# Row-packed score matmuls: each head of a pair in its own half of TensorE's rows, on two PSUM banks at once

## The chip, the cores and the metric

One NeuronCore of a Trainium2 chip runs the whole program. The metric is the device time of one execution in microseconds, the median of several. Engines: PE is TensorE, DVE VectorE, ACT ScalarE, POOL GpSimd, SP SyncE, whose queue issues the DMAs.

## What is computed

Input x is 16 batches of 512 tokens of 256 values. The part that matters is the attention of 16 heads of 16 values each; the rest is cut.

```python
scores = jnp.take(causal_kern, jnp.maximum(doff, 0), axis=-1)
...
scores = scores + qm[..., :, None] + km[..., None, :]
qc = (x @ cq_w).reshape(Bq, Sq, H, CR).transpose(0, 2, 1, 3)
kc = (x @ ck_w).reshape(Bq, Sq, H, CR).transpose(0, 2, 1, 3)
scores = scores + MIX * jnp.einsum('bhic,bhjc->bhij', qc, kc) / math.sqrt(CR)
scores = jnp.where(causal, scores, -1000000000.0)
attn = jax.nn.softmax(scores, axis=-1)
ctx = jnp.einsum('bhij,bhjd->bhid', attn, v)
...
s = attention block with its FFN of 1024;  g = silu(FP4-rounded gated FFN of 704)
x = x + s * g
```

## The kernel before

A preparation (weights rounded to FP4 values and transposed, the positional kernel of all batches) is followed by a program over batches in three parts: a head (batch 0 and what must precede it), a loop over batches 1 to 14, and an end. Each engine runs a list of steps in an order written out by hand in the table `ORDER`, one string per engine and part, so that the work of three neighbouring batches is interleaved: the attention and the gated FFN of batch b, the output projection and the wide FFN of batch b-1, and the projections and the first half of the maxima of batch b+1. Steps wait for each other by counted semaphores (`Event`).

The score of a head is a bf16 matmul. Queries and keys (8 values a head) are split in three bf16 parts and laid out in 48 rows of products, with 6 more rows for the bias terms and, for the scores, 2 rows for a shift (minus the row maximum). A pair of heads shares one block of `KS` (keys): 2 x 54 rows. `QS` (queries) has one block per head, in which the other head's rows are zero, so that a matmul over 108 rows (L563, maxima) or 112 rows (L591 and L595, scores) gives one head's result. POOL zeroes QS at the end of the preparation (L1251).

The steps that the change touches:
- `mx.half.pair.unit`: raw scores of query tiles against all earlier keys, on PE (L563) into one of two banks (3 and 4) of PSUM. DVE reduces them to row maxima (L927, with a memset of an unused column, L922, ahead). A pair has five units in `MAXUNITS`, each of one bank: (512), (384 and 128), twice, and (256 and 256).
- `sc.pair.unit`: the transposed scores. A head has three units: its four own diagonal blocks of 128 columns (L591), and two of past blocks, 384 and 256+128 columns (L595). Each takes the next of two banks (0 and 1). ACT exponentiates them (L740 in place, L749 into `Pr`). The own blocks are then multiplied with the positional weights `Tz` by DVE (`muld`, L957), which is what frees their bank; the past blocks are multiplied by POOL (`mul`, L1062) in SBUF.
- `pv`: probabilities times values of four heads (L611), fp32, four heads on four strips of 32 columns of the array, into one bank.
- `load`: SP loads KS and QS of half of the pairs from DRAM, six DMAs (L492). `mio` brings the shift rows.

Other PE steps go to four more banks. L683 and L692 are the wide FFN, L635 and L650 the gated one, L665 the output projection, L542 and L550 the projections of x, L571 the transposes of the shifts.

The waits for a bank look like this (before): a score unit waits for the one two units ago.

```python
n = 6 * p + u
ago = n - len(SC_BANKS)
```

Of the kernel before, what the change touches and what calls it, by code (L numbers as in the profile page):

```python
# [40 lines left out]
KROWS = 2 * (HROWS + BROWS)  # L41
SHIFT = 2
SROWS = KROWS + 2 * SHIFT
# [1524 lines left out]
```

How the kernel before makes its waits and increments, by code:

```python
    def wait(self, eng, b, k=None):  # L63
        if isinstance(b, int) and b < 0:
            return
        k = self.per - 1 if k is None else k
        eng.wait_ge(self.sem, b * (self.per * self.by) + (k + 1) * self.by)
# [1125 lines left out]
        def prologue_sync(sp):  # L1194
            sp.dma_start(freqs, w["waves"]).then_inc(L["waves"], 16)
            sp.dma_start(pos, w["positions"]).then_inc(L["waves"], 16)
            for i in range(NX):
                sp.dma_start(x_in[i][:], x_b[i]).then_inc(x_sem[i], 16)
            sp.wait_ge(L["zero"], N_MEMSETS)
            for dst, src in zero_list:
                sp.dma_start(dst, src).then_inc(L["consts"], 16)
            for dst, src in load_list:
                sp.dma_start(dst, src).then_inc(L["weights"], 16)
            with sp.Fori(1, B // NX) as n:
                for i in range(NX):
                    sp.wait_ge(L["pool"], n * NX + (i - NX + 1))
                    sp.dma_start(x_in[i][:], x_b[n * NX + i]).then_inc(x_sem[i], 16)
            sp.dma_start(rows_d.rearrange("b h n -> (b h) n").rearrange("(p a) n -> p a n", a=2)[:, :, S:ROW],
                         zeros.rearrange("p (a n) -> p a n", a=2)).then_inc(L["rows"], 16)
            sp.wait_ge(L["exp"], 1)
            for g in range(4):
                sp.dma_start(rows_d[:, g::4, 0:S], dens[32 * g:32 * g + B]).then_inc(L["rows"], 16)
            sp.wait_ge(L["ready"], 5)
            sp.dma_start(qb_d[:, 0:3, :], KS[0:H, 0:3, :]).then_inc(L["ones"], 16)
```

## Time and profile before

| | |
|---|---|
| median of 3 runs | 2038.28 us (2036.96 to 2039.29) |
| the profiled execution, its own time | 2039.16 us |
| its span, first to last instruction | 2037.4 us |
| busy: PE, DVE, POOL, ACT | 1852.7, 1611.7, 1106.1, 900.0 us |
| mean granted clock of TensorE | 0.959 of full speed |

Busy time counts the time in which at least one instruction of an engine runs. A matmul's duration holds its passage through the array, so durations of neighbouring matmuls overlap; what a matmul costs the next is read from start to start. "PEld" rows are weight loads. "issue" is time in which nothing that the profile shows was waited for.

### The profile page before, as it was taken

Reading aid. Unit: us, or ns where it says so; the run is one execution under the profiler, and the core shown is the slowest. Engines: PE = TensorE matmul, PEld = TensorE weight load, DVE = VectorE, ACT = ScalarE, POOL = GpSimd, SP = SyncE. Lnnn points to the kernel's source line nnn. Section 1 sums busy time; section 2 is a strip of 40 time slices with the busy share of each in tenths; the row PEclk is TensorE's granted clock in tenths of the full one; section 3 lists DMA queues with packets and bytes.
Section 4 is the critical chain, followed back from the end, with each engine's and each line's share of the span. In section 5 each row is a group of like instructions: output and inputs, shape, how many; then the busy total and the mean of one; then the engine's idle time right before and its main releaser. Section 6 shows DMA issues by size and latency. Waiting matters only on the chain.

```text
span 2037.4 us, 41650 instructions
## 1 busy us (share of the span) xinstructions
PE 1852.7 (91%) x12508; PEld 1316.0 (65%) x12508; DVE 1611.7 (79%) x5186; ACT 900.0 (44%) x1814; POOL 1106.1 (54%) x788
## 2 busy tenths in 40 slices
PE   4745789999999999999999999999999999999996
PEld 1222356767676776767676767767676767677765
DVE  5863987888888888978888888889788888888752
ACT  0111345445453635454454536354544545364532
POOL 1223464746564665747465646657474656466471
PEclk7757899999999999999999999999999999999998
DMA  7204122323232222223232322232232323222110
GB/s 215 85 11 111 36 79 71 114 71 102 60 102 70 86 68 86 87 70 112 70 102 60 103 70 85 68 87 87 70 112 70 102 60 101 72 84 68 52 64 21
DMA packets 129139, 165.32 MB, mean 81 GB/s; under 512 B 9821, under 2 KB 90718, under 8 KB 129028
## 3 DMA queue, kind: packets, MB, share of 16 engines
q1 hardware_dynamic: 129034, 164.29, 28.0%
q14 instruction: 84, 0.69, 0.1%
q8 instruction: 21, 0.34, 0.1%
HBM read 127.85 MB, written 36.41 MB: 81 GB/s over the span
## 4 chain that ended last, share of the span: by engine, by line
PE 57%; DVE 13%; issue 12%; POOL 5%; ACT 2%; DMA 1%; DVEq 0%; ACTq 0%; POOLq 0%; SPq 0%
PE ps L692 10%; PE ps L683 10%; PE ps L635 8%; PE ps L542 4%; PE ps L650 4%; PE ps L563 3%; PE ps L665 3%; PE ps L595 3%; POOL Pr L1062 3%; PE ps L550 2%; PE ps L611 2%; PE ps L591 2%; DVE st L859 2%; DVE nmax L927 2%; POOL slot L1094 1%
## 5 line engine op out<-in xcount | busy, mean ns | idle before, releaser
L1062 POOL TENSOR_TENSOR Pr<-Pr,Tz 128x768 f32<-128x768 f32 (+2 forms) x384 | 478.2, 1274 | 251.6 <-ACT Pr L749 249.8
L927 DVE CUSTOM_DVE_ANT_0 ps<-ps,future 128x512 f32<-128x512 f32 (+3 forms) x1024 | 474.8, 517 | 50.1 <-issue 49.7
L749 ACT ACTIVATE Pr<-ps 128x384 f32<-128x384 f32 x512 | 243.3, 489 | 373.7 <-PE ps L595 371.0
L683 PE MATMUL ps<-catT,w 128*128 128x256 f32 x1024 | 237.3, 380 | 0.7 <-ACT catT L810 0.7
L563 PE MATMUL ps<-KS,QS 108*128 108x512 bf16 (+3 forms) x1024 | 220.6, 306 | 17.2 <-DVE nmax L927 11.4
L692 PE MATMUL ps<-w,gT 128*128 128x256 f32 x1024 | 233.0, 381 | 0.9 <-ACT gT L821 0.9
L740 ACT ACTIVATE ps<-ps 128x512 f32<-128x512 f32 x256 | 150.4, 587 | 147.9 <-PE ps L591 145.9
L957 DVE SCALAR_TENSOR_TENSOR Pr<-ps,Tz 128x512 f32<-128x512 f32 x256 | 175.2, 685 | 46.7 <-ACT ps L740 40.3
L692 PEld LDWEIGHTS ps<-w,gT 128*128 128x128 f32 x1024 | 190.9, 190 | 25.8 <-ACT gT L821 1.3
L683 PEld LDWEIGHTS ps<-catT,w 128*128 128x128 f32 x1024 | 189.7, 190 | 26.7 <-ACT catT L810 1.0
L635 PE MATMUL ps<-wgT,xqT 128*128 128x352 f32 x512 | 178.7, 472 | 3.6 <-DVE slot L994 2.9
L650 PE MATMUL ps<-wdT,hqT 128*128 128x256 f32 x768 | 178.5, 382 | 0.9 <-ACT hqT L786 0.9
L595 PE MATMUL ps<-QS,KS 112*128 112x384 bf16 (+2 forms) x768 | 161.9, 275 | 19.0 <-DVE Pr L957 14.2
L635 PE MATMUL ps<-wuT,xqT 128*128 128x352 f32 x512 | 174.6, 464 | 0.0
L1094 POOL TENSOR_TENSOR slot<-slot 128x704 f32<-128x704 f32 x64 | 107.7, 1683 | 99.6 <-DVE slot L849 99.6
L1100 POOL TENSOR_TENSOR rstd<-ve,minus_half 128x4 f32<-128x4 f32 x32 | 32.6, 1019 | 232.9 <-DVE ve L867 231.4
L650 PEld LDWEIGHTS ps<-wdT,hqT 128*128 128x128 f32 x768 | 142.7, 190 | 20.4 <-ACT hqT L786 1.4
L611 PE MATMUL ps<-Pr,v_cur 128*17 128x128 f32 (+2 forms) x3584 | 151.0, 319 | 0.1
L563 PEld LDWEIGHTS ps<-KS,QS 108*128 108x128 bf16 x1024 | 88.0, 98 | 92.3 <-DVE nmax L927 41.6
L927 DVE DVE_READ_ACCUMULATOR2_ANT nmax<- 128x1 f32 x1024 | 144.0, 141 | 0.0
L635 PEld LDWEIGHTS ps<-wuT,xqT 128*128 128x128 f32 x512 | 98.2, 192 | 55.2 <-issue 1.7
L611 PEld LDWEIGHTS ps<-Pr,v_cur 128*17 128x17 f32 x3584 | 94.6, 97 | 52.1 <-issue 39.4
(214 smaller groups left out, 3262.1 us busy)
## 6 DMA issues: line engine op xcount, KB each, us to landing
Tz<-kernel_rows SPq DMA_DIRECT2D x128, 512.0 KB, 3.8
KS<-k_parts SPq DMA_DIRECT2D x32, 384.0 KB
QS<-q_parts SPq DMA_DIRECT2D x64, 192.0 KB
hY<-in_x SPq DMA_DIRECT2D x20, 512.0 KB, 4.9
xn<-in_x SPq DMA_DIRECT2D x20, 512.0 KB, 3.5
out<-y SPq DMA_DIRECT2D x16, 512.0 KB, 3.0
q_parts<-q_sp SPq DMA_DIRECT2D x16, 384.0 KB, 2.8
k_parts<-k_sp SPq DMA_DIRECT2D x16, 384.0 KB, 2.4
```

The source lines that it names most:

```text
L563: ins = mm(o, QS[0:KROWS, 2 * p + e, it * P:(it + 1) * P], KS[0:KROWS, p, 0:n], start=True, stop=True)
L595: ins = mm(dst[:, at:at + PAST[j]], KS[0:SROWS, p, j * P:(j + 1) * P], rhs[:, S - 1:P * (j + 1) - 1:-1], start=True, stop=True)
L611: ins = mm(dst[32 * hh:32 * hh + HD + 1, to:to + n], v_cur[:, j, 4 * g + hh, :], rhs[:, n - 1::-1], start=i == 0, stop=i == len(pieces) - 1)
L635: ins = mm(dst[:, 0:IH], xqT[:, c, t * P:(t + 1) * P], wt[:, c, f * IH:(f + 1) * IH], start=c == 0, stop=c == KD - 1)
L650: ins = mm(dst[:, 0:D], hqT[:, c * P:(c + 1) * P], wdT[:, c, :], start=c == 0, stop=c == KI - 1)
L683: ins = mm(dst[:, i * n:(i + 1) * n], w1[:, c, f * P:(f + 1) * P], catT[:, c, hf * n:(hf + 1) * n], start=c == 0, stop=c == KD - 1)
L692: ins = mm(dst[:, 0:D], gT[:, f, at:at + P], w2[:, f, :], start=f == 0, stop=f == KF - 1)
L740: inc(af(src, src, ACT.Exp), "a_exp")
L749: inc(af(Pr[:, p % 4, e, at:at + wd], src[:, 0:wd], ACT.Exp), "a_exp")
L927: ins = v.tensor_tensor_reduce(o, o, future[:, S - n:S], -1.0, 3e38, ALU.add, ALU.min, nmax[:, 2 * pl + e, it:it + 1])
L957: v.scalar_tensor_tensor(blocks(Pr[:, p % 4, e, 0:S]), blocks(ps[:, SC_BANKS[n % len(SC_BANKS)], :]), 3e38, near, ALU.min, ALU.mult).then_ ...
L1062: ins = g.tensor_tensor(a, a, Tz[:, p % 2, :, P * j:P * j + PAST[j]], ALU.mult)
```

## The change

Each head of a pair gets rows of its own: the first rows 0 to 55, the second rows 64 to 119, in both QS and KS. QS has one block per pair, without zeros. A matmul takes 54 (maxima) or 56 rows (scores) at row 0 or 64, and the two heads' matmuls of a block are written one after the other. The unit of a step is now a pair: it takes two banks, one per head, and counts one PE event at its last matmul. A pair has three units of maxima (512; 384 and 128; 256; each for both heads) and three of scores (own; 384; 256+128). ACT and DVE count an event per bank. Ring lengths stay: two banks for scores, two for maxima. The loads are eight DMAs a half. POOL's memset of QS is gone. The table `ORDER` is another one for all engines and parts.

```diff
-KROWS = 2 * (HROWS + BROWS)
+KROWS = HROWS + BROWS
 SHIFT = 2
-SROWS = KROWS + 2 * SHIFT
+SROWS = KROWS + SHIFT
+HALF_ROWS = P // 2
...
-MAXUNITS = [[(0, 3)], [(0, 2), (0, 0)], [(1, 3)], [(1, 2), (1, 0)], [(0, 1), (1, 1)]]
+MAXUNITS = [[3], [2, 0], [1]]
+NM, NS = len(MAXUNITS), 1 + len(UNITS)
...
-        QS = sb("QS", [P, H, S], BF16)
+        QS = sb("QS", [P, PAIRS, S], BF16)
...
-        NLOAD = 6
+        NLOAD = 8
...
                     for e in range(2):
-                        r0, r1 = e * HROWS, 2 * HROWS + e * BROWS
-                        loads += [(QS[r0:r0 + HROWS, heads, :][:, e::2, :], rows(qs_d, 2 * CR)[r0:r0 + HROWS]),
-                                  (QS[r1:r1 + BROWS, heads, :][:, e::2, :], rows(qb_d, 2)[e * BROWS:(e + 1) * BROWS])]
+                        r = HALF_ROWS * e
+                        for t, parts_d, bias_d in ((KS, ks_d, kb_d), (QS, qs_d, qb_d)):
+                            loads += [(t[r:r + HROWS, pairs, :], rows(parts_d, 2 * CR)[e * HROWS:(e + 1) * HROWS]),
+                                      (t[r + HROWS:r + KROWS, pairs, :], rows(bias_d, 2)[e * BROWS:(e + 1) * BROWS])]
...
-                    dst = b_bank(s)
+                    dst = []
                     at = 0
-                    for e, it in MAXUNITS[u]:
+                    for it in MAXUNITS[u]:
                         n = (it + 1) * P
-                        o = dst[:, at:at + n]
-                        ins = mm(o, QS[0:KROWS, 2 * p + e, it * P:(it + 1) * P], KS[0:KROWS, p, 0:n], start=True, stop=True)
+                        for e in range(2):
+                            if len(dst) == e:
+                                dst.append(b_bank(s + (e,)))
+                            r = slice(HALF_ROWS * e, HALF_ROWS * e + KROWS)
+                            ins = mm(dst[e][:, at:at + n], QS[r, p, it * P:(it + 1) * P], KS[r, p, 0:n], start=True, stop=True)
                         at += n
                     inc(ins, "pe_max")
...
+                    for j in range(T) if u == 0 else UNITS[u - 1]:
+                        wd = P if u == 0 else PAST[j]
+                        hi, lo = (P * j + P - 1, P * j - 1) if u == 0 else (S - 1, P * (j + 1) - 1)
+                        for e in range(2):
+                            if len(dst) == e:
+                                n = 2 * (NS * p + u) + e
+                                ago = n - len(SC_BANKS)
...
+                                if ago // 2 % NS == 0:
+                                    v_mul[ago % 2].wait(pe, hb, ago // 2 // NS)
+                                else:
+                                    E["a_exp"].wait(pe, hb, ago)
+                                dst.append(ps[:, SC_BANKS[n % len(SC_BANKS)], :])
+                            r = slice(HALF_ROWS * e, HALF_ROWS * e + SROWS)
+                            rhs = QS[r, p, hi::-1] if lo < 0 else QS[r, p, hi:lo:-1]
+                            ins = mm(dst[e][:, at:at + wd], KS[r, p, j * P:(j + 1) * P], rhs, start=True, stop=True)
+                        at += wd
                     inc(ins, "pe_sc")
...
-            g.memset(QS[:].rearrange("p h s -> p (h s)").bitcast(F32), 0.0).then_inc(L["ready"], 1)
```

Two places of the loop show how the order moves on PE. In the rows, KS and QS are the score operands, `v_max` tells that DVE has read a maxima bank, `a_exp` that ACT has read a score bank, `v_mul0` and `v_mul1` that DVE's product has freed one.

PE, the last stretch of the loop before the change: maxima of the last two pairs (L563), P times V (L611) between them.

```order
L563 MATMUL ps<-KS,QS 128x512 [waits v_max]
...
L563 MATMUL ps<-KS,QS 128x384 [waits v_max]
L563 MATMUL ps<-KS,QS 128x128
L611 MATMUL ps<-Pr,v_cur 17x384 [waits g_mul,v_gs,v_mul1,a_vcopy]
L611 MATMUL ps<-Pr,v_cur 17x384 x3
L611 MATMUL ps<-Pr,v_cur 17x256 x4
L611 MATMUL ps<-Pr,v_cur 17x128 x20
...
L563 MATMUL ps<-KS,QS 128x512 [waits v_max]
```

PE, the same stretch now: L543 are the maxima, L575 the scores, L590 P times V.

```order
L575 MATMUL ps<-QS,KS 128x384 [waits v_mul0]
L575 MATMUL ps<-QS,KS 128x384 [waits v_mul1]
...
L543 MATMUL ps<-KS,QS 128x384 [waits v_max]
...
L543 MATMUL ps<-KS,QS 128x384 [waits v_max]
L543 MATMUL ps<-KS,QS 128x128 x2
L575 MATMUL ps<-QS,KS 128x256 [waits a_exp] x2
L575 MATMUL ps<-QS,KS 128x128 x2
...
L543 MATMUL ps<-KS,QS 128x256 [waits v_max]
...
L543 MATMUL ps<-KS,QS 128x512 [waits v_max]
...
L543 MATMUL ps<-KS,QS 128x384 [waits v_max]
...
L590 MATMUL ps<-Pr,v_cur 17x384 [waits g_mul,v_gs,v_mul1,a_vcopy]
```

Units of two banks stand one behind another here, each waiting for the banks of the one before. (Of the last three units the second head's rows are left out at "...".)

PE, early in the loop, before the change:

```order
L591 MATMUL ps<-QS,KS 128x128 [waits a_exp]
L591 MATMUL ps<-QS,KS 128x128 x3
...
L673 MATMUL ps<-ident,hY 128x128 x3
...
L595 MATMUL ps<-QS,KS 128x384 [waits a_exp]
...
L563 MATMUL ps<-KS,QS 128x384 [waits v_max]
L563 MATMUL ps<-KS,QS 128x128
...
L595 MATMUL ps<-QS,KS 128x256 [waits v_mul0]
```

and now:

```order
L575 MATMUL ps<-QS,KS 128x128 x6
...
L652 MATMUL ps<-ident,hY 128x128 x3
...
L543 MATMUL ps<-KS,QS 128x512 [waits v_max]
...
L575 MATMUL ps<-QS,KS 128x384 [waits v_mul0]
L575 MATMUL ps<-QS,KS 128x384 [waits v_mul1]
...
L543 MATMUL ps<-KS,QS 128x384 [waits v_max]
...
L575 MATMUL ps<-QS,KS 128x256 [waits a_exp]
```

The scores of 384 columns now wait for both products of the unit just before; before, they had a bank that was one unit older. Runs of score and maxima matmuls alternate with full-array work as they did.

## Rows read from the trace of the kernel before

**Rows 1.** the page, busy times (share, instructions) and PE's busy tenths in 40 slices
```profile
PE 1852.7 (91%) x12508; PEld 1316.0 (65%) x12508; DVE 1611.7 (79%) x5186; ACT 900.0 (44%) x1814; POOL 1106.1 (54%) x788
...
PE   4745789999999999999999999999999999999996
```

**Rows 2.** windows of one batch each, all engines; first line: the columns
```profile
core 0: us, PE busy (x) PEld busy (x) DVE busy (x) ACT busy (x) POOL busy (x), PEclk, DMA share, GB/s
...
983.60:1095.70 112.10, 108.66 (x766) 79.37 (x765) 93.73 (x305) 54.99 (x110) 66.30 (x47) 1.00 0.28 83
...
sum 560.50, PE 543.29 PEld 396.56 DVE 468.60 ACT 274.98 POOL 331.44; mean PE 108.66 PEld 79.31 DVE 93.72 ACT 55.00 POOL 66.29
```

**Rows 3.** timeline of PE: start us, us, instructions, idle before
```profile
1007.40 1.89 PE L683 MATMUL ps<-catT,w 128*128 128x256 f32 x8
1009.13 0.60 PE L563 MATMUL ps<-KS,QS 108*128 108x512 bf16 x3
1009.57 1.95 PE L683 MATMUL ps<-catT,w 128*128 128x256 f32 x8
...
1011.79 0.49 PE L595 MATMUL ps<-QS,KS 112*128 112x384 bf16 x3
1012.21 2.36 PE L611 MATMUL ps<-Pr,v_cur 128*17 128x384 f32 x56
1014.50 0.40 PE L591 MATMUL ps<-QS,KS 112*128 112x128 bf16 x4
```

**Rows 4.** weight loads by shape: count, busy us, mean ns, idle before
```profile
L692 PEld LDWEIGHTS ps<-w,gT 128*128 128x128 f32 x1024 | 190.9, 190 | 25.8 <-ACT gT L821 1.3
...
L611 PEld LDWEIGHTS ps<-Pr,v_cur 128*17 128x17 f32 x3584 | 94.6, 97 | 52.1 <-issue 39.4
...
L563 PEld LDWEIGHTS ps<-KS,QS 108*128 108x128 bf16 x1024 | 88.0, 98 | 92.3 <-DVE nmax L927 41.6 <-issue 11.8 <-DVE v_new L911 3.4
```

**Rows 5.** timeline of all engines, handoffs of score units
```profile
1000.46 0.69 DVE L957 SCALAR_TENSOR_TENSOR Pr<-ps,Tz 128x512 f32<-128x512 f32 x1
...
1001.20 0.34 PE L595 MATMUL ps<-QS,KS 112*128 112x256 bf16 x2 [0.45 <-DVE Pr L957]
1001.28 0.89 ACT L749 ACTIVATE Pr<-ps 128x384 f32<-128x384 f32 x2
...
1001.85 0.40 PE L591 MATMUL ps<-QS,KS 112*128 112x128 bf16 x4 [0.31 <-ACT Pr L749]
...
1002.28 0.58 ACT L740 ACTIVATE ps<-ps 128x512 f32<-128x512 f32 x1
```

**Rows 6.** timeline of DVE, maxima one behind another
```profile
1082.76 0.72 DVE L927 CUSTOM_DVE_ANT_0 ps<-ps,future 128x512 f32<-128x512 f32 x1
...
1083.41 0.59 DVE L927 CUSTOM_DVE_ANT_0 ps<-ps,future 128x384 f32<-128x384 f32 x1
...
1083.92 0.33 DVE L927 CUSTOM_DVE_ANT_0 ps<-ps,future 128x128 f32<-128x128 f32 x1
...
1084.18 0.46 DVE L927 CUSTOM_DVE_ANT_0 ps<-ps,future 128x256 f32<-128x256 f32 x1
...
1084.55 0.14 DVE L927 DVE_READ_ACCUMULATOR2_ANT nmax<- 128x1 f32 x1
```

**Rows 7.** waits of PE and its loads, one batch: us, times, longest
```profile
PE ps L595 <- DVE Pr L957: 0.7, 2, 0.4
...
PEld ps L595 <- DVE Pr L957: 1.6, 3, 0.7
PEld ps L563 <- DVE nmax L927: 1.5, 5, 0.5
```

**Rows 8.** timeline of the end of the preparation
```profile
152.05 3.51 POOL L1251 MEMSET QS<- 128x4096 f32 x1
...
156.19 0.18 DVE L1383 MEMSET slot<- 128x64 f32 x2 [7.08 <-ACT wdT L1467]
...
159.99 0.35 SPq L1217 DMA_DIRECT2D q_bias_parts<-KS  x1
```

More of the change, by code:

```diff
@@ L180 @@
         sync="""
-            last:T.0 last:load.1 last:T.1 last:T.2 last:T.3 last:mio.1 last:T.4 last:T.5 last:T.6 last:T.7 last:fin
+            last:T.0 last:load.1 last:T.1 last:T.2 last:T.3 last:T.4 last:mio.1 last:T.5 last:T.6 last:T.7 last:fin
             tail:fin
@@ L279, in b_uses @@
 def b_uses(s):
-    return [s] if s[0] in ("xT", "proj", "v", "mx", "mT") else []
+    return [s + (e,) for e in range(2)] if s[0] == "mx" else [s] if s[0] in ("xT", "proj", "v", "mT") else []
 def build(nc, x_d, w, out_d):
@@ L500, in sync_steps @@
                     for e in range(2):
[L501 to L503 removed]
+                        r0 = HALF_ROWS * e + KROWS
+                        sp.dma_start(QS[r0:r0 + SHIFT, HALF * half:HALF * (half + 1), :], sd[e]
+                                     ).then_inc(d_shift[half].sem, 16)
                 elif k == "T":
@@ L914, in vector_steps @@
                     _, half, pl, u = s
-                    E["pe_max"].wait(dve, half_batch(half, b), 20 * half + 5 * pl + u)
-                    src = bank(b_plan, s)
+                    E["pe_max"].wait(dve, half_batch(half, b), (half * HALF + pl) * NM + u)
                     if pl == 0 and u == 0:
@@ L921, in vector_steps @@
                             E["v_m"].wait(dve, b, 3)
-                    v.memset(turn[:, 20 * half + 5 * pl + u:20 * half + 5 * pl + u + 1], 0.0)
-                    at = 0
-                    for e, it in MAXUNITS[u]:
-                        n = (it + 1) * P
-                        o = src[:, at:at + n]
-                        ins = v.tensor_tensor_reduce(o, o, future[:, S - n:S], -1.0, 3e38, ALU.add, ALU.min,
-                                                     nmax[:, 2 * pl + e, it:it + 1])
-                        at += n
-                    inc(ins, "v_max")
+                    n0 = (half * HALF + pl) * NM + u
+                    v.memset(turn[:, n0:n0 + 1], 0.0)
+                    for e in range(2):
+                        src = bank(b_plan, s + (e,))
+                        at = 0
+                        for it in MAXUNITS[u]:
+                            n = (it + 1) * P
+                            o = src[:, at:at + n]
+                            ins = v.tensor_tensor_reduce(o, o, future[:, S - n:S], -1.0, 3e38, ALU.add, ALU.min,
+                                                         nmax[:, 2 * pl + e, it:it + 1])
+                            at += n
+                        inc(ins, "v_max")
                 elif k == "mfin":
@@ L933, in vector_steps @@
                     hb = half_batch(half, b)
-                    E["v_max"].wait(dve, hb, 20 * half + 19)
+                    E["v_max"].wait(dve, hb, 2 * (half + 1) * HALF * NM - 1)
                     if half:
```

295 lines of the change are left out of this document (124 added, 171 removed).

## Prediction

> **What bounds the kernel now.** I read the page's busy shares and slices first, then the windows of one batch, then PE's groups by shape, then the timeline of PE. The page: PE is busy 91% of the span, DVE 79%, and from slice 7 on PE's digit is 9 [rows 1]. Batches 1 to 14 run in one loop. Its period is 112.10 us, the same in each window; of it PE is busy 108.7, DVE 93.7, ACT 55.0, POOL 66.3, and the granted clock is 1.00, the upper level of 2.4 GHz, 0.417 ns a column [rows 2]. So PE sets the batch, with 3.4 us in which nothing at all is in flight on it.
>
> The score matmuls are bf16 and stream a column a clock: three of them (512, 384 and 128 columns) start at 1009.13 and the next matmul at 1009.57, 0.44 us for 1024 columns [rows 3]. A head has 1280 columns of maxima (L563) and 1280 of scores (L591, L595), a batch 16 x 2560 = 40960 columns = **17.1 us of PE's 112.1**.
>
> **Does packing overlap at all?** The trace has one packed case. P times V (L611) puts four heads on four column strips: 56 passes of 128 to 384 columns end in 2.36 us [rows 3]. One head alone is 1280 columns, in two passes at two clocks a column (fp32; L683 x8 of 256 columns takes 1.73 us to the next start, 0.84 ns a column [rows 3]), 2.13 us. So four strips cost what one does, and I take it that two row halves do likewise: **-8.5 us a batch**. Bounds: 0 (they serialize), and -8.5.
>
> Weights could forbid it, since each matmul has a load of its own. A bf16 load of 128 columns takes 98 ns, no more than an fp32 one of 17 columns (97); an fp32 one of 128 takes 190 [rows 4], 0.84 ns a column over the 17. So 97 ns is nearly all latency, an fp32 load of 128 streams in about 107 ns and the bf16 one in some 15. Two bf16 loads fit behind the shortest pair (53 ns) if row halves keep that speed.
>
> **What it costs on PE: switches.** Where PE goes from full-array matmuls to strips of 32 columns and back, time is lost. L595 x3 starts at 1011.79 with 768 columns (0.32), P times V starts at 1012.21, not 1012.11; its last column passes near 1014.41 (1012.21 + 2.13, and about 5 ns for each of its 14 steps), and L591 starts at 1014.50. Both ways 0.095 us, against under 0.01 us between full-array matmuls of any two kinds (1009.13 to 1009.57) [rows 3]. The 14 switches of a batch before (four P times V, two transposes of shifts, one 32-column projection) are 1.3 us. In the changed kernel every run of maxima or scores is in a third shape, 64 rows by 128 columns. Counted down the order, the loop has 60 changes of shape where it had 14, because these runs are short and lie between full-array work: 46 x 0.095 = **+4.4 us a batch**; bounds 0 (row halves switch free) and +4.4. The Trainium skill, "TensorEngine Tiling (Array Packing)", Key Properties, says that changing the tiling mode, not just the tile, drains TensorE. By that rule row halves pay like strips, and the trace agrees for strips; without it the sum would be lower by 4.4 us a batch.
>
> **What it costs in waits: rings of one.** Before, a score unit took one of banks 0 and 1, a maxima unit one of 3 and 4: PE filled one while ACT or DVE emptied the other. Now a unit takes both banks, so PE's next unit of that kind waits until the last is emptied, and the consumer then waits for PE. From rows: four matmuls of 128 columns (L591 at 1001.85) last 0.40 where their columns need 0.22, so a result is 0.17 late; ACT starts 0.03 after it (1002.25, 1002.28), PE 0.05 after DVE (1001.15, 1001.20); ACT takes 0.58 for 512 columns, 0.89 for two units of 384, DVE's product 0.69 [rows 5]. DVE's maxima take from start to start 0.65 for 512 columns, 0.51 for 384, 0.26 for 128, 0.37 for 256, and 0.14 for the last readout [rows 6]. From PE's last column to the release of the second bank this makes 1.7 us (512), 1.9 (384 and 128), 1.2 (256), 1.2 (scores of 384) and 2.3 (own-block scores with the product; 1.6 for the first bank). PE's own work between two units of a kind must be that long. At the loop's end it isn't. Scores 256+128 follow 0.2 after the unit they reuse: wait 1.0. Then maxima 256 wait 0.75, maxima 512 wait 1.2, maxima 384+128 wait 1.7: together 4.7 us within three runs. Near the start, scores 384 after own-block scores and maxima 384+128 wait 1.6 more, other places 0.8. Walking the whole order so, with DVE and ACT free whenever wanted, gives 7.1 us; the same walk down the order of before, with two banks in turn, 1.4. **+5.7 us a batch**, bounds +3 (handoffs quicker, waits that swallow a switch) and +8 (DVE late as well).
>
> The trace of before has such waits, small: in one batch PE's weight loads are held 1.6 us for DVE's products and 1.5 for its maxima, and of the first only 0.7 shows on PE itself [rows 7]; the rest lies behind the ends of running matmuls. DVE's lateness adds about 2 us to the walk's 1.4 before; I assume the same afterwards, since DVE has as much to do (40 memsets become 24, -1 us, hidden: DVE isn't the bound). ACT and POOL do the same work. SP issues 8 loads a half instead of 6, with the same bytes; no wait of PE for a DMA is among the waits of a batch [rows 7], so I cost it at nothing, and if that cover went it would be the issue of four DMAs a batch.
>
> **Outside the loop.** POOL's memset of QS goes (3.51 us); behind it stand the memset of KS, that of v_new, and at 159.99 the first DMA that waits for them. DVE's memset ends at 156.4, so this DMA moves by 3.4 [rows 8]: **-3.4 us**, once. Batch 0 and batch 15 lie in the head and end: each -8.5 for pairs, +2.4 and +3.7 for 25 and 38 more switches. In the head the first half's maxima run with DVE back to back, and a round trip of some 0.45 us for each of 12 units comes on top (+5); the end has ring waits like a batch. I put both at 0, bounds -6 and +6 each.
>
> **Sum.** A batch: -8.5 + 4.4 + 5.7 = +1.6 (I take +1.5: 0.1 for switches swallowed in waits). 14 x 1.5 = +21, less 3.4: +17.6 on the profiled execution's 2039.16 us, which lies inside the runs of before (median 2038.28): **2056 us**, +0.9%.
>
> **Rivals.**
> 1. *Faster: the waits stay small.* The order is new for all engines, and other work may cover the round trips (DVE has 18 us idle a batch [rows 2]); then a batch is 112.1 - 8.5 + 4.4 = 108.0, and with -3.4 and -6 in each of head and end the time is 2039 - 57 - 15 = 1967. It decides where ring waits grow by less than 4.1 us a batch. For it: before, PE's own wait for DVE's products is 0.7 us a batch [rows 7]. Against: at the loop's end the four units stand almost side by side and no cover is in the order. If switches are free as well, another 62 off: 1905.
> 2. *Pairs overlap only in part.* If row halves lose the fast bf16 load, a pair with loads of 107 ns each lasts at least 214 ns: 48 pairs of 128 columns go from 112 to 214 (+4.9), 16 of 256 stay, 16 of 384 gain 1.7, 8 of 512 gain 1.7: a batch +1.5 where I have -8.5, 2056 + 160 = 2216, somewhat less as PE's slower pace fills waits. With plain serial pairs: +8.5 x 16 = 136, 2190.
> 3. *Slightly partial overlap*, a quarter of the 8.5 lost: +34, 2090. The Trainium skill, "TensorE: Matmul & The Clock Gate", Packing small matmuls, gives 3.07 times for four row tiles of 512 columns; at that efficiency two give 1.54 instead of 2, and the sum would be 6.0 for pairs in place of 8.5, some 40 us more. No run here shows it; the strips of L611 show none of it.
> 4. *The change doesn't do what it says*: the matmuls of a pair might stand apart. The order shows them next to each other, each with its own bank's wait. I give it nothing of its own.
>
> **Chances.** Forecast (2035 to 2080) 0.5; rival 1 in some strength 0.31; rival 3 0.1; rival 2 0.09. The likeliest gives the time. Two in ten left out, the range reaches half way into rival 1 and over rival 3: **1985 to 2100**. A measurement here tells 0.2% (4 us) from no change. Faster 0.31, same 0.08, slower 0.61. The forecast's own range is 2035 to 2080.
>
> **What would show it.** Overlap: the starts of a pair's two matmuls under 0.02 us apart, and a pair of 512 columns 0.22 us to the next start. Switches: 0.095 us between the last pair's columns and a full-array matmul, some 60 times a batch. Rings: PE or its loads waiting for DVE's maxima by 3 to 6 us a batch, most of it in the last 12 us of the loop. DVE busy near 93 us of a longer period. q_bias_parts' first DMA near 156.6. I'm wrong if the period is under 111.9, if a pair's starts lie a whole stream apart, or if switches of 64-row shapes cost nothing.

## The result: 3.2% slower, and the profile after

The changed kernel takes **2104.42 us** (median of 4 runs, 2099.68 to 2105.24) against 2038.78 (2036.96 to 2039.46) of the kernel before on the same chip: ratio 1.0319, 95% interval 1.0301 to 1.0336. Slower was forecast, but by 18 us, not 66; the time lies just above the range.

The profiled execution took 2104.96 us, its span is 2103.1. The page, to be held against [rows 1]:

```profile
PE 1883.8 (90%) x12508; PEld 1230.9 (59%) x12508; DVE 1597.2 (76%) x4930; ACT 924.6 (44%) x1844; POOL 1095.3 (52%) x787
...
PEclk8757689999999999999999999999999999999998
...
L543 PE MATMUL ps<-KS,QS 54*128 54x512 bf16 (+3 forms) x1024 | 188.2, 322 | 70.7 <-DVE nmax L907 68.5
```

PE is 31 us busier, though its columns are fewer; its maxima (L543) wait 68.5 us for DVE, where those of the kernel before (L563) waited 11.4. The slices' clock digit still reads 9 all through the loop, which hides what follows. Three batches, beside [rows 2]:

```profile
core 0: us, PE busy (x) PEld busy (x) DVE busy (x) ACT busy (x) POOL busy (x), PEclk, DMA share, GB/s
1008.10:1124.00 115.90, 110.44 (x765) 74.00 (x765) 92.95 (x289) 56.55 (x113) 65.89 (x47) 0.97 0.30 80
1124.00:1241.00 117.00, 111.55 (x766) 74.52 (x766) 92.89 (x289) 56.61 (x113) 65.91 (x47) 0.96 0.29 80
1241.00:1356.70 115.70, 110.24 (x765) 73.52 (x766) 92.81 (x289) 56.55 (x113) 65.93 (x47) 0.97 0.29 81
```

The period is 116.2 in the mean of 14 (1627.1 us) where it was 112.1 (1569.7), and **the granted clock is 0.96 or 0.97 where it was 1.00**. Cut into stretches of 6.8 us at the loop's end, the same view shows where (the last row is the 3.4 us just ahead of the fall):

```profile
1105.80:1112.60 6.80, 4.92 (x25) 2.58 (x24) 6.13 (x25) 2.13 (x5) 4.95 (x4) 1.00 0.00 0
1112.60:1119.40 6.80, 5.80 (x62) 3.10 (x63) 5.17 (x20) 0.20 (x1) 5.09 (x4) 0.50 0.00 1
1119.40:1126.20 6.80, 5.89 (x37) 4.48 (x36) 2.28 (x10) 3.26 (x7) 1.45 (x1) 1.00 0.24 81
...
1109.20:1112.60 3.40, 1.75 (x9) 0.48 (x7) 3.20 (x17) 1.39 (x4) 2.74 (x3) 1.00 0.00 0
```

For 6.8 us TensorE runs at the lower of its two levels (0.50, 1.2 GHz), once in every batch; in 4 of the 14 a second fall of 3.4 us follows near the loop's start. In the 3.4 us ahead of the fall shown PE was busy for 1.75. PE's timeline over the place:

```profile
1108.82 0.39 PE L543 MATMUL ps<-KS,QS 54*128 54x384 bf16 x3 [0.23 <-DVE nmax L907]
...
1110.18 0.28 PE L543 MATMUL ps<-KS,QS 54*128 54x256 bf16 x1 [0.45 <-DVE nmax L907]
1110.95 0.28 PE L543 MATMUL ps<-KS,QS 54*128 54x256 bf16 x1 [0.49 <-DVE nmax L907]
1111.82 0.77 PE L543 MATMUL ps<-KS,QS 54*128 54x512 bf16 x2 [0.59 <-DVE nmax L907]
1113.45 1.25 PE L543 MATMUL ps<-KS,QS 54*128 54x384 bf16 x4 [0.86 <-DVE nmax L907]
1114.67 4.47 PE L590 MATMUL ps<-Pr,v_cur 128*17 128x384 f32 x56
```

Each maxima unit waits until DVE has emptied both banks of the last. These are the ring waits that were forecast, at the place that was forecast. What was not: the clock falls among them, and P times V (56 passes, L590) takes 4.47 us where it takes 2.36 [rows 3].

**The ledger of a batch.** All kernels below are compared in one way: over the 14 loop batches, the time from each matmul's start to the next is split into its columns at full clock; what is over at a change of shape, up to 0.105 us (switches); what is over otherwise by more than 0.02 us (waits); and what a stretch at half clock adds (clock). Such a stretch is called a fall below. Us a batch; the four add up to the period within 0.1.

| kernel | columns | switches | waits | clock | period | run, us |
|---|---|---|---|---|---|---|
| before | 103.9 | 1.4 | 6.9 | 0 | 112.1 | 2038.8 |
| changed | 96.1 | 5.8 | 11.3 | 3.0 | 116.2 | 2104.4 |
| full_paired | 103.5 | 1.4 | 10.0 | 2.3 | 117.2 | 2124.3 |
| light_max | 95.7 | 5.8 | 12.0 | 2.5 | 116.1 | 2089.7 |
| light_mul | 96.0 | 5.8 | 11.3 | 2.8 | 116.0 | 2103.2 |
| light_both | 95.8 | 5.8 | 9.7 | 1.5 | 112.8 | 2046.7 |
| full_light | 103.6 | 1.4 | 9.9 | 1.9 | 116.8 | 2109.3 |
| full_both | 103.7 | 1.4 | 7.9 | 0.2 | 113.2 | 2057.3 |
| before_both | 103.8 | 1.4 | 5.9 | 0 | 111.1 | 2014.0 |
| before_slow | 103.9 | 1.4 | 8.0 | 0 | 113.2 | 2056.8 |
| before_slower | 103.8 | 1.4 | 9.9 | 0.6 | 115.8 | 2101.5 |
| halves_single | 98.4 | 7.8 | 19.9 | 3.7 | 129.9 | 2310.4 |
| spread_end | 96.3 | 6.0 | 12.6 | 4.2 | 119.0 | 2145.7 |
| spread_both | 96.0 | 6.2 | 18.2 | 7.4 | 127.9 | 2270.6 |
| early7 | 96.3 | 6.1 | 13.7 | 3.1 | 119.3 | 2150.1 |
| sc7_early | 96.1 | 6.1 | 14.9 | 7.9 | 125.1 | 2234.3 |

The periods are those of the profiled execution, the last column is the median of all; for before_slower the two lie apart, since its profiled execution took 2087.3, the fastest of five, and the others had a lower mean clock (0.953 to 0.955 against 0.959). The clock column is the least certain: in the changed kernel batches with 10.2 us at half clock last 117.0 to 117.5 and those with 6.8 last 115.7 to 116.0, some 1.1 us for 3.4, by which the 7.8 us a batch at half clock would cost 2.5 and not 3.0.

So the change moves a batch by -7.8 (columns) + 4.4 (switches) + 4.4 (waits) + 3.0 (clock) = +4.1, 57 us over the loop. The rest of the 65.7 us between the two spans lies behind it: from the loop's end to the last instruction 165.9 us against 156.9, and 310.1 against 310.8 ahead of the loop's first whole batch.

### The profile page after: what moved, and what is told of

Read it like the earlier page. It is cut to its first block, busy times and chain, and to the rows that moved or that the text cites. A ratio compares the mean times of both kernels' runs of the same rounds, so it can differ in the third digit from the quotient of the medians.

```text
span 2103.1 us, 40843 instructions
## 1 busy us (share of the span) xinstructions
PE 1883.8 (90%) x12508; PEld 1230.9 (59%) x12508; DVE 1597.2 (76%) x4930; ACT 924.6 (44%) x1844; POOL 1095.3 (52%) x787
## 4 chain that ended last, share of the span: by engine, by line
PE 59%; DVE 20%; issue 10%; ACT 1%; DVEq 0%; POOL 0%; DMA 0%; ACTq 0%; POOLq 0%; SPq 0%
PE ps L662 11%; PE ps L671 11%; PE ps L590 7%; DVE ps L907 6%; PE ps L614 6%; PE ps L629 4%; PE ps L519 4%; PE ps L575 3%; PE ps L644 3%; PE ps L527 3%; PE ps L543 2%; DVE nmax L907 2%; PE ps L622 2%; DVE slot L974 2%; DVE Pr L937 2%
## 5 line engine op out<-in xcount | busy, mean ns | idle before, releaser
L727 ACT ACTIVATE Pr<-ps 128x384 f32<-128x384 f32 x512 | 222.7, 487 | 296.2 <-PE ps L575 294.9
L543 PE MATMUL ps<-KS,QS 54*128 54x512 bf16 (+3 forms) x1024 | 188.2, 322 | 70.7 <-DVE nmax L907 68.5
L662 PE MATMUL ps<-catT,w 128*128 128x256 f32 x1024 | 246.5, 393 | 0.3 <-ACT catT L788 0.3
L1068 POOL TENSOR_TENSOR slot<-slot,sc_h 128x704 f32<-128x704 f32 x64 | 88.9, 1389 | 273.9 <-DVE sc_h L816 273.9
L937 DVE SCALAR_TENSOR_TENSOR Pr<-ps,Tz 128x512 f32<-128x512 f32 x256 | 168.4, 685 | 23.3 <-ACT ps L723 20.5
L575 PE MATMUL ps<-QS,KS 56*128 56x128 bf16 (+2 forms) x1792 | 166.7, 248 | 21.6 <-DVE Pr L937 11.7
L590 PE MATMUL ps<-Pr,v_cur 128*17 128x128 f32 (+2 forms) x3584 | 183.8, 364 | 0.1
L723 ACT ACTIVATE ps<-ps 128x512 f32<-128x512 f32 x256 | 137.3, 579 | 86.0 <-PE ps L575 85.7
L543 PEld LDWEIGHTS ps<-KS,QS 54*128 54x128 bf16 x1024 | 54.6, 95 | 179.3 <-DVE nmax L907 130.2
L590 PEld LDWEIGHTS ps<-Pr,v_cur 128*17 128x17 f32 x3584 | 106.8, 109 | 76.7 <-issue 63.5
```

The lines of the kernel that those rows point to most:

```text
L543: ins = mm(dst[e][:, at:at + n], QS[r, p, it * P:(it + 1) * P], KS[r, p, 0:n], start=True, stop=True)
L575: ins = mm(dst[e][:, at:at + wd], KS[r, p, j * P:(j + 1) * P], rhs, start=True, stop=True)
L590: ins = mm(dst[32 * hh:32 * hh + HD + 1, to:to + n], v_cur[:, j, 4 * g + hh, :], rhs[:, n - 1::-1], start=i == 0, stop=i == len(pieces) - 1)
L662: ins = mm(dst[:, i * n:(i + 1) * n], w1[:, c, f * P:(f + 1) * P], catT[:, c, hf * n:(hf + 1) * n], start=c == 0, stop=c == KD - 1)
L723: inc(af(src, src, ACT.Exp), "a_exp")
L727: inc(af(Pr[:, p % 4, e, at:at + wd], src[:, 0:wd], ACT.Exp), "a_exp")
```

## The experiments

Two theories stood after the first trace. **A**: the clock falls after waits of PE that lie close together, whatever makes them; the row halves have no part in it. **B**: it falls because of work in row halves, with its 60 changes of shape. Lines of code and of order are shortened in the edits below; "..." marks what is left out.

### 1. The new order without row halves (full_paired)

```diff
-KROWS = HROWS + BROWS
+KROWS = 2 * (HROWS + BROWS)
...
-r = slice(HALF_ROWS * e, HALF_ROWS * e + KROWS)
-ins = mm(dst[e][:, at:at + n], QS[r, p, it * P:(it + 1) * P], KS[r, p, 0:n], start=True, stop=True)
+ins = mm(dst[e][:, at:at + n], QS[0:KROWS, 2 * p + e, it * P:(it + 1) * P], KS[0:KROWS, p, 0:n],
```

> The changed kernel's order, its two-bank units and its rings of one, but the score operands have all 128 rows again (108 or 112 used, a head's other rows zero), so no pair overlaps and the loop has 14 changes of shape as before. Theory A (the time that my sum missed is a lower granted clock, which follows the short waits of PE at the loop's end; the row halves have no part in it): PE's granted clock falls to half here too, once or twice a batch after those waits; a batch is 103.9 of columns + 1.4 of switches + 10 to 11 of waits + 2.6 to 3.9 of clock = 118 to 120 us (116.1 in the changed kernel, 112.1 before), 2120 to 2150 us in all. Theory B (the clock falls because of the work in row halves, with its 60 changes of shape): no fall in the loop, a batch of 115.5 to 116.5, 2085 to 2100 us.

2124.33 us, ratio 1.0432 (1.0414 to 1.0449), a batch of 117.2. At the loop's end, the timeline and two windows:

```profile
1236.20 0.28 PE L542 MATMUL ps<-KS,QS 108*128 108x256 bf16 x1 [0.62 <-DVE nmax L907]
1236.96 0.28 PE L542 MATMUL ps<-KS,QS 108*128 108x256 bf16 x1 [0.48 <-DVE nmax L907]
1237.84 0.77 PE L542 MATMUL ps<-KS,QS 108*128 108x512 bf16 x2 [0.59 <-DVE nmax L907]
1239.47 1.36 PE L542 MATMUL ps<-KS,QS 108*128 108x384 bf16 x4 [0.86 <-DVE nmax L907]
```

```profile
1232.30:1239.10 6.80, 4.31 (x22) 2.22 (x20) 6.10 (x26) 2.13 (x5) 5.59 (x4) 1.00 0.00 0
1239.10:1245.90 6.80, 6.29 (x64) 3.37 (x65) 4.53 (x18) 0.60 (x1) 5.00 (x4) 0.50 0.00 1
```

The same waits with 108 rows, and the same fall of 6.8 us (3.4 in 5 of the 14 batches). B is refuted for the clock; A stands, its batch somewhat below the 118 to 120 expected. The order and the two-bank units together cost 5.1 us a batch (waits +3.1, clock +2.3); row halves give 1.0 of it back. No run takes the new order apart from the rings of one: that these waits come from the rings rests on the rows above, where each unit waits for DVE to empty the banks of the one before.

### 2. Row halves in the order of before (halves_single)

```diff
-MAXUNITS = [[(0, 3)], [(0, 2), (0, 0)], [(1, 3)], [(1, 2), (1, 0)], [(0, 1), (1, 1)]]
+MAXUNITS = [[(0, 3)], [(0, 2), (0, 0)], [(1, 3)], [(1, 2), (1, 0)], [(0, 1)], [(1, 1)]]
...
-rhs = QS[0:SROWS, 2 * p + e, :]
+r = slice(HALF_ROWS * e, HALF_ROWS * e + SROWS)
+rhs = QS[r, p, :]
...
-ins = mm(dst[:, at:at + PAST[j]], KS[0:SROWS, p, j * P:(j + 1) * P],
+ins = mm(dst[:, at:at + PAST[j]], KS[r, p, j * P:(j + 1) * P],
```

> The order of the kernel before, a unit of one head in one of two banks in turn, but with each head's operands on a row half of its own (54 and 56 rows from row 0 or 64); the maxima unit that held blocks of both heads is split in two. The loop has 81 changes of shape where it had 15, and only where units of two heads stand side by side can they overlap. Both theories: 66 x 0.095 = +6.3 us a batch for the switches, 0 to -1.5 for neighbours that overlap, +0 to +1 for the waits. Theory A (clock follows the waits): clock stays at 1.00 in the loop, a batch of 117 to 119 us, 2110 to 2135 us in all. Theory B (clock follows row halves): it falls to half for some 7 us a batch or more, a batch of 120 to 123 us, 2150 to 2190 us. If a switch costs less where nothing overlaps, the batch is under 115.

2310.40 us, ratio 1.1348 (1.1329 to 1.1367). Switches came out as expected (7.8 against 1.4, 0.097 each). Two things did not. Columns fell by 5.5, far more than I allowed: a unit of one head starts while another head's is running, whatever their kinds. In this timeline of PE score units of the two heads both start at 1326.45, and a maxima matmul at 1326.62 runs beside a score matmul at 1326.63:

```profile
1326.45 0.28 PE L598 MATMUL ps<-QS,KS 56*128 56x256 bf16 x1 [0.24 <-DVE Pr L960]
1326.45 0.28 PE L594 MATMUL ps<-QS,KS 56*128 56x128 bf16 x2
...
1326.62 0.27 PE L565 MATMUL ps<-KS,QS 54*128 54x256 bf16 x1
1326.63 0.22 PE L594 MATMUL ps<-QS,KS 56*128 56x128 bf16 x1
...
1332.35 0.61 PE L565 MATMUL ps<-KS,QS 54*128 54x512 bf16 x1 [5.39 <-DVE nmax L930]
```

And waits rose to 19.9, as I read it for a reason of my own making: the split unit makes six units a pair out of five, so PE gets only two shorter units ahead of DVE, and here it waits 5.39 us through a long stretch of DVE's other work. (In that batch PE also waits 1.1 us for a load of QS.) The run tells nothing of the clock apart from waits (both are high), and only the switch price and the overlap are to be kept from it.

### 3. Moving the waits apart by order (spread_end, spread_both)

```diff
-dn.1 sc.7.0 mx.0.1.2 ctxt.2 tr.2.1 mx.0.2.0 dn.2 sc.7.1 mx.0.2.1 sc.7.2 mx.0.2.2 mx.0.3.0 mx.0.3.1 pv.3 tr.3.0 tr.3.1 mx.0.3.2 ctxt.3 dn.3
+dn.1 sc.7.0 mx.0.1.2 ctxt.2 tr.2.1 mx.0.2.0 sc.7.1 mx.0.2.1 sc.7.2 dn.2 mx.0.2.2 mx.0.3.0 pv.3 mx.0.3.1 tr.3.0 tr.3.1 ctxt.3 mx.0.3.2 dn.3
```

(dn is the down projection of the gated FFN and tr the transposes ahead of it, hr the rounding of its hidden values, f1 the first product of the wide FFN, ctxt a transpose behind P times V.) spread_both also has `mx.1.1.0 f1.0.0 sc.1.1 mx.1.1.1 f1.0.1 sc.1.2 xT.0 xT.1 sc.2.0` near the start.

> The changed kernel with only PE's order at the loop's end written otherwise: dn.2 stands behind the second and third of the last five maxima units, pv.3 between the fourth and the fifth, so fewer units stand side by side. Theory A: the waits there fall by 1 to 2 us a batch, and the clock no longer falls at the loop's end (2.6 to 3.4 us a batch given back): a batch of 111 to 113 us, 2035 to 2065 us in all. Theory B: the clock falls as before, at the same place or another: a batch of 114 to 115, 2075 to 2095 us. A third way: the waits only move to the product of POOL that pv.3 needs, and neither falls: 2095 to 2110.

> As the last one, and the tight place near the loop's start (four score and maxima units around hT) is spread with f1.0.0, f1.0.1 and the two transposes of x as well. Theory A: another 0.8 us of waits and the second, shorter fall of the clock (3.4 us of half clock in some batches) go: 1 to 2 us a batch below spread_end, a batch near 110.5, 2020 to 2050 us in all, level with the kernel before or faster. Theory B: only the waits fall, 2065 to 2085 us.

2145.65 (ratio 1.0543, 1.0524 to 1.0562) and 2270.64 (1.1112, 1.1051 to 1.1172): both far above every band. sc.7.1, put ahead of dn.2, waits 2.2 us for DVE's product of the last pair, because DVE does 1.9 us of hr.3 between the two products of that pair; near the start f1.0.0 waits 2.4 us a batch for a bank that DVE's gate product (slot, L973) has still to empty, and a maxima unit behind it 3.8 for ACT's eviction of the transposed x. The waits rose, and the clock with them (4.2 and 7.4 a batch). The versions don't test what they were made for; in them the two rose together, but light_max below shows that this is no rule.

### 4. Shorter waits without touching PE (light_max, full_light)

```diff
-o = src[:, at:at + n]
-ins = v.tensor_tensor_reduce(o, o, future[:, S - n:S], ...)
+o = src[:, at:at + P]
+ins = v.tensor_tensor_reduce(o, o, future[:, S - n:S - n + P], ...)
```

In light_max DVE takes the row maxima over the first 128 columns of each block alone; the maxima over its other columns are left out. full_light is full_paired with the same edit.

> The changed kernel with every instruction of PE, ACT and POOL as it is; DVE's maxima read 128 columns of each block in place of its 128 to 512, so a part of the maxima is left out. Per head DVE's reductions fall by 0.4 (512), 0.25 (384) and 0.1 (256) us, the ring of one is released that much sooner. Theory A (the clock follows PE's waits): waits fall from 11.4 to 8 or 9 us a batch and the clock no longer falls: 96.2 + 5.8 + 8.5 = 110.5 to 111.5 us a batch (116.1 in the changed kernel), 2025 to 2045 us in all. If the clock falls all the same with the waits gone (it follows what PE executes): 113 to 114.5 a batch, 2060 to 2085 us.

> The same light maxima in the kernel with full-array operands of the first experiment (117.2 us a batch there). With waits and clock out of the way the two differ by pairs and switches alone: -7.3 of columns and +4.5 of switches in row halves make a batch 3 us longer here than in light_max. Theory A: clock 1.00, 103.5 + 1.4 + 8 = 113 to 114 us a batch, 2055 to 2080 us in all, 35 to 50 us over light_max. If the difference is under 15 us, switches or pairs are mis-sized.

2089.67 (1.0258, 1.0238 to 1.0277) and 2109.27 (1.0354, 1.0334 to 1.0373). DVE is busy 82.4 us a batch in place of 92.9, and the period of light_max stays at 116.1. PE's and POOL's timeline at the loop's end of light_max:

```profile
1446.68 0.64 PE L543 MATMUL ps<-KS,QS 54*128 54x512 bf16 x2 [0.45 <-DVE nmax L907]
1447.78 0.64 PE L543 MATMUL ps<-KS,QS 54*128 54x384 bf16 x4 [0.46 <-DVE nmax L907]
1451.13 4.47 PE L590 MATMUL ps<-Pr,v_cur 128*17 128x384 f32 x56 [2.71 <-POOL Pr L1042]
```

```profile
1446.81 4.07 POOL L1042 TENSOR_TENSOR Pr<-Pr,Tz 128x768 f32<-128x768 f32 x3 [0.59 <-ACT Pr L727]
```

PE reaches its last maxima unit 2 us sooner (103.3 us into the batch, not 105.4) and then waits 2.7 us for **POOL's product of the last pair**, the second chain: scores, exp, DVE's product, scores again (their ring is of one too), exp, POOL. In the changed kernel it ended at 1114.41, 0.26 before P times V started; the maxima waits hid it. My expectation had one chain only: light_max lies 45 us above its band, full_light 29, and the two are 20 us apart, not 35 to 50. In light_max the waits are more than in the changed kernel (12.0 against 11.3) and the clock costs less (2.5 against 3.0), so the sum of the waits doesn't set the clock.

### 5. Both chains shortened, or the second alone (light_both, light_mul)

```diff
-for j in range(T - 1):
+for j in range(1 if p == 7 else T - 1):
```

light_both is light_max with this line in POOL's product, which leaves out two of its three parts for the last pair of each batch; light_mul has this line alone.

> light_max again, and POOL's product of the last pair of a batch is made for the first of its three parts only (the other two left out), so both things that PE waits for at the loop's end are short: in light_max PE went through the maxima sooner and then waited 2.8 us for that product, and a batch stayed at 116.0. Theory (two chains end there together, DVE's maxima by rings of one and scores, exp, product of the last pair; each hides the other): waits fall from 12.0 to 8 or 9 us a batch and, the waits being what the clock follows, the clock stays at 1.00: 110 to 112 us a batch, 2005 to 2035 us in all. If the clock follows what PE executes, 2.5 more a batch, 2045 to 2070. If a third chain stands behind, over 2075.

> The changed kernel with the full maxima and that short product of POOL. By the same theory the maxima alone hold PE to the same point (in the changed kernel the product ended at 1114.41 and PE's last maxima matmul at 1114.6): waits 10 to 11.4 a batch, clock falling as before, 115 to 116.1 us a batch, 2085 to 2104 us in all. If the product was what bound and the maxima only filled its time: under 113 a batch, under 2065.

2046.68 (1.0048, 1.0031 to 1.0065) and 2103.23 (1.0327, 1.0309 to 1.0344). The product alone gives nothing, the maxima alone 15 us, both 58 (the chips differ; by the ratios 13 and 55): two chains of nearly equal length end at P times V. With PE's instructions unchanged, 11.3 us of waits become 9.7 and the fall of 6.8 us becomes one of 3.4:

```profile
1428.80:1541.40 112.60, 108.64 (x765) 73.03 (x764) 81.61 (x289) 56.46 (x113) 64.07 (x45) 0.98 0.31 83
```

So the clock isn't set by what PE executes alone; shorter waits gave half of the fall back. It didn't come back to 1.00 as A had it: waits of 2.8 us in all are still there in the 8 us ahead of P times V. And though 11 us of DVE's and 2 of POOL's work are gone, it is still slower than before.

### 6. Waits put into the kernel before (before_slow, before_slower)

```diff
+if half == 0 and pl == 3:
+    at0 = 80 * e + 4 * it * (it + 1)
+    for i in range(8 * (it + 1)):
+        v.memset(slow[:, at0 + i:at0 + i + 1], 0.0)
 ins = v.tensor_tensor_reduce(o, o, future[:, S - n:S], ...)
```

That is before_slower; before_slow has 2 * it + 3 of them, in the last two pairs.

> The kernel before with one thing added: ahead of the maxima of the last two pairs of a batch DVE also writes 3, 5, 7 or 9 single columns of zeros, 5 to 6 us more of DVE's time in the last stretch of the loop. PE's instructions, their order, the full array and the two banks in turn stay. Theory A (waits of PE close together lower the clock, whatever makes them): PE waits 3 to 5 us more a batch and the clock falls to half there for some 7 us, 2.5 to 3.4 us more: a batch of 118 to 120.5 us, 2120 to 2155 us in all. A rival (the clock falls only with the changed order or with two-bank units): clock 1.00, a batch of 115 to 117, 2080 to 2110 us.

> As before_slow (which cost only 1.1 us of waits a batch and no clock), but stronger and in one place: in the last pair of a batch alone DVE writes 8 columns of zeros, some 0.06 us each, for each 128 columns of maxima that it then reads, 9 to 10 us more in the last five maxima units. Theory A (waits of PE close together lower the clock whatever makes them): 5 to 7 us more of waits and the clock at half for 3.4 to 7 us, 1.5 to 3.4 us more: a batch of 119 to 123 us, 2130 to 2185 us in all, with full-array operands, two banks in turn and the order of before. Rival (the new order or the two-bank units lower it): clock 1.00, 117 to 119 a batch, 2105 to 2135 us.

2056.82 (1.0095, 1.0075 to 1.0115) and 2101.47 (1.0325, 1.0308 to 1.0343). Two banks in turn swallow most of it: waits +1.1 and, in the usual batch of before_slower, +2.3, at clock 1.00. But in 6 of its 14 batches the period is over 116, and in these six, and in no other, the clock falls for 3.4 us:

```profile
1119.00:1238.80 119.80, 110.33 (x766) 80.22 (x765) 98.63 (x465) 55.22 (x110) 66.76 (x47) 0.99 0.27 78
1238.80:1353.20 114.40, 108.73 (x765) 79.36 (x764) 96.18 (x465) 54.95 (x110) 66.22 (x47) 1.00 0.28 82
```

The batch ahead of these two:

```profile
1114.33 0.39 PE L572 MATMUL ps<-ident_bf,sh_sp 128*16 128x128 bf16 x4 [1.78 <-DVE sh_sp L947]
1114.65 4.54 PE L651 MATMUL ps<-wdT,hqT 128*128 128x256 f32 x12
```

Here the clock falls at 1115.0, behind waits of 0.88 (at 1109.66) and 1.78 us, and the down projection takes 4.54 us; two more batches fall so. In the other three, each the next one behind such a batch, it falls about where a single wait of 3.54 us for hY ends. All with full-array operands, one-bank units and the order of before: the rival of this run is refuted. The size was under what I expected.

But the second batch of the two windows has the same two waits and no fall (clock 1.00):

```profile
1345.53 0.39 PE L564 MATMUL ps<-KS,QS 108*128 108x384 bf16 x2 [0.88 <-DVE nmax L932]
...
1350.20 0.39 PE L572 MATMUL ps<-ident_bf,sh_sp 128*16 128x128 bf16 x4 [1.78 <-DVE sh_sp L947]
```

So A holds in its weak form: waits can bring the fall in any of these kernels, and the same waits don't always.

### 7. The last candidates for a better version (early7, sc7_early)

```diff
-muld.7.0 hr.3 muld.7.1 mx.0.2.0 ...          DVE
+muld.7.0 muld.7.1 mx.0.2.0 hr.3 ...
-... mx.0.2.0 dn.2 sc.7.1 mx.0.2.1 sc.7.2 mx.0.2.2 mx.0.3.0 mx.0.3.1 pv.3 ...     PE
+... mx.0.2.0 sc.7.1 dn.2 sc.7.2 mx.0.2.1 mx.0.2.2 pv.3 mx.0.3.0 ...
-mul.6 hr.3 mul.7          POOL
+mul.6 mul.7 hr.3
```

That is sc7_early, whose POOL product also starts its first part one exp unit sooner; early7 differs: on PE xqT is moved there and dn.2 stands behind sc.7.2, on DVE dn.1 and ctxt.2 move too, and POOL's product starts as before.

> The changed kernel with the end of its loop ordered otherwise on four engines: DVE's two products of the last pair directly after each other, xqT moved from the middle to between sc.7.0 and sc.7.1, so that sc.7.2 comes ahead of dn.2, POOL's last product ahead of hr.3, and pv.3 between maxima units. If the waits at the end come from the order alone, they fall by 1 to 2 us a batch and by theory A the clock stays up: 112 to 114 us a batch, 2050 to 2080 us in all. If DVE is what binds there (it is busy over nine tenths of the last 20 us of the loop), the waits move only: 115 to 117 a batch, 2090 to 2120 us, with the clock falling as before.

> A version meant to compute all: the changed kernel with both chains at the loop's end made shorter by order. DVE's second product of the last pair ahead of hr.3, sc.7.1 ahead of dn.2, sc.7.2 directly behind it, POOL's last product ahead of hr.3 with its first part started when the exps of sc.7.1 are there, pv.3 ahead of the last three maxima units. By the rows the product ends some 2.5 us sooner and a part of the maxima moves behind pv.3: waits fall by 1.5 to 3 us a batch, and if that keeps the clock up 2.6 more: 111 to 114 us a batch, 2035 to 2080 us in all. If DVE binds through the stretch, the waits move behind pv.3: 115 to 117, 2090 to 2120.

2150.10 (1.0556, 1.0532 to 1.0579) and 2234.29 (1.0955, 1.0929 to 1.0982). The product did come sooner, but waits rose elsewhere (a maxima unit 1.7 us at 1667.63 of sc7_early, where the kernel had none) and in 8 of the 14 batches of sc7_early the clock fell four times. The few lines of order that I changed broke more than they mended.

### 8. What row halves are worth with short waits (full_both, before_both)

The two light edits in full_paired and in the kernel before: again the maxima beyond 128 columns of a block and two thirds of POOL's last product are left out.

> The order, two-bank units and rings of one of the changed kernel on full-array operands, with both light chains as in light_both (112.6 us a batch): DVE's maxima over 128 columns of each block, POOL's last product for its first part only; both parts left out. If pairs (-7.7) and 46 switches (+4.5) are what the trace says, a batch here is 3.2 us longer, less what the slower columns cover of the waits and of the clock: 114 to 116, 2065 to 2100 us in all, 25 to 50 us over light_both. If a switch costs more than its 0.097 us (through the waits behind it), the two come out within 15 us.

> The kernel before with the same two light chains (maxima over 128 columns of each block, the last product's first part only; both parts left out). It is bound by PE and waits 6.9 us a batch, of which DVE's lateness is about 2: 110.5 to 111.8 us a batch, 2010 to 2035 us in all, clock 1.00. What full_both lies above it is the new order with its two-bank units, even with short waits: 2.5 to 5 us a batch, 35 to 70 us.

2057.30 (1.0100, 1.0083 to 1.0117) and 2013.95 (0.9899, 0.9876 to 0.9922). From before_both to full_both: +2.1 us a batch, all of it waits (+2.0) and a rare fall of the clock: the price of the new order and units where DVE and POOL are quick, below my 2.5 to 5. From full_both to light_both I expected 1.5 to 3.5 us less a batch and 25 to 50 us in all; it is 0.4, and 10.6 us between the two runs, inside the 15 that I had set as the sign of dearer switches:

```profile
1435.50:1548.40 112.90, 108.96 (x764) 79.65 (x764) 82.77 (x289) 56.56 (x113) 64.12 (x45) 1.00 0.29 82
```

Not because a switch costs more than 0.097: columns are -7.9 and switches +4.5, as traced. Waits (+1.8) and clock (+1.3) take 3.1 of the 3.4. As I read it, a PE that is quicker reaches DVE's and ACT's unfinished work sooner, and the clock falls after that; no run tests this by itself.

## Why the prediction was wrong

The sign and the three mechanisms named held, the size didn't: 2104 against 2056, because a fourth, the clock, had no term. By its steps:

- **Pairs, -8.5 a batch**: -7.8. Most pairs overlap wholly. In a timeline of the changed kernel,

```profile
1096.77 0.34 PE L575 MATMUL ps<-QS,KS 56*128 56x384 bf16 x2
1096.94 0.38 PE L543 MATMUL ps<-KS,QS 54*128 54x512 bf16 x2
1097.26 2.36 PE L590 MATMUL ps<-Pr,v_cur 128*17 128x384 f32 x56
```

two heads' 384 columns take 0.17 us to the next start and two of 512 take 0.32 with the switch, 0.22 without: one head's time each. Rivals 2 and 3 are out. For two row tiles of 512 columns the factor is about 2, not the 1.54 that I had worked out in rival 3 from the Trainium skill's figure for four ("TensorE: Matmul & The Clock Gate", Packing small matmuls).
- **Switches, +4.4**: +4.4 (81.5 us in 840 changes, 0.097 each; 19.0 in 196 before). The rule of the Trainium skill, "TensorEngine Tiling (Array Packing)", Key Properties, that a change of mode drains TensorE, is borne out for row halves as for strips: the time is lost with no regard to which mode follows which.
- **Ring waits, +5.7 (3 to 8)**: +4.4, at the places named, most of it in the last 20 us of a batch. The walk came this near in part by luck: "DVE and ACT free whenever wanted" and "ACT and POOL do the same work" left the second chain out. POOL's last product ended at nearly the same moment as the maxima, so it added nothing, and shorter maxima would have gained little.
- **The step that failed** is that the batch's clock is 1.00 [rows 2] and stays there; it had no term and no bound. It costs 3.0 us a batch, 42 us over the loop. The spans' difference (65.7) exceeds the 17.6 forecast by 48: +42 for the clock, +10 for pairs, -18 for ring waits, +1 for the 0.1 swallowed, +9 for the end and +3 ahead of the loop make 47. The loop of before shows no fall, but behind the loop its trace has three. A row that I had read for the end gave 0.93 there, and I drew nothing from it. That row, PE's timeline at the first of the falls, and two windows:

```profile
1880.50:2037.40 156.90, 131.72 (x845) 102.06 (x843) 81.64 (x243) 60.42 (x122) 68.17 (x47) 0.93 0.16 47
```

```profile
1893.56 0.40 PE L591 MATMUL ps<-QS,KS 112*128 112x128 bf16 x4 [0.42 <-ACT Pr L749]
...
1895.36 0.34 PE L595 MATMUL ps<-QS,KS 112*128 112x256 bf16 x2 [1.08 <-DVE Pr L957]
...
1896.28 0.50 PE L595 MATMUL ps<-QS,KS 112*128 112x384 bf16 x1 [0.36 <-ACT Pr L749]
```

```profile
1892.80:1896.20 3.40, 1.62 (x15) 0.80 (x12) 3.40 (x14) 2.40 (x7) 0.00 (x0) 1.00 0.00 0
1896.20:1899.60 3.40, 3.17 (x13) 2.27 (x13) 2.46 (x7) 3.05 (x6) 2.36 (x1) 0.50 0.00 0
```

Waits of 0.42 and 1.08 us, and during a third of 0.36 the clock falls; PE was busy for 1.62 of the 3.4 us ahead, 1.75 in the changed kernel: the same picture, in the kernel before. A change that adds 5 us of waits in one place should have had a bound for the clock from these rows.
- **The end, 0 (-6 to +6)**: +9.0, outside its bounds: waits +10.4, clock +3.2, switches +3.7, columns -6.0, and 2.2 less behind the last matmul. It has the same rings, and I set it at 0 without walking it.
- **Preparation and head, -3.4 and 0**: together -0.7. The first q_bias_parts DMA was forecast at 156.6, and the timeline has it at

```profile
155.21 0.35 SPq L1197 DMA_DIRECT2D q_bias_parts<-KS  x1
```

4.8 sooner than [rows 8]: 3.4 as forecast, and 1.3 because POOL comes to these memsets that much sooner (150.73, not 152.05), in work that the change doesn't touch. So what lies between this DMA and the loop came out some 4 longer, within the head's bounds; which part of it isn't separated.
- **Costed at nothing**: SP's 8 loads: PE has no wait for a DMA in the loop (three of 1.0 us in all before). DVE busy 92.9 of a longer period, as said.

In sum: -7.8 + 4.4 + 4.4 + 3.0, by the periods +4.1 a batch, where -8.5 + 4.4 + 5.7 - 0.1 = +1.5 stood. Without the clock it is +1.1, by this ledger, and the forecast would have been some 6 us off in the loop.

**What stays open.** How the falls start exactly (which waits, how close) I can't tell: kernels with like waits in a batch differ (before_slow 8.0 and none, full_both 7.9 and two in 14 batches), and so do batches of one kernel with the same waits (before_slower). Whether the ring waits come from the two-bank units alone or in part from the new order is open too. Whether another order of the changed kernel beats the kernel before is open as well; four attempts by hand were slower, and no run gave a version that computes all and beats 2038.

## What to carry to other kernels

A matmul made quicker is worth its time only as long as nothing else fills the gap: here the pairs took 7.8 us off PE's columns as planned, and changes of shape, rings of one and the clock took 11.8 back. Packing that takes both banks of a ring for one unit leaves PE no bank to fill meanwhile; count the round trip of every consumer and each chain that ends at the same place before the columns. And where an edit adds idle time of PE in one place, give the granted clock a term: with the clock at half, the work behind the wait costs up to twice (P times V 4.47 us in place of 2.36).

## What the hardware showed that I had not expected

- The clock falls in the midst of a loop in which PE is 95% busy, among or right behind short waits of PE (five of 0.23 to 0.86 us at 1108.8 to 1113.5 of the changed kernel; 0.88 and 1.78 in before_slower), and stays at half for 3.4 or 6.8 us, with the full array as with row halves. The same waits in another batch of before_slower brought no fall.
- A change of shape costs 0.097 us on average, in each direction, between strips, row halves and the full array alike (medians of the six directions, away from half clock: 0.093 to 0.098).
- Matmuls on different row halves overlap also when they belong to different kinds of work and to different units (1326.45 and 1326.62 in halves_single). Each unit here writes a bank of its own; one shared bank was not tried.
